# The expert layers' result stores move from SyncE's queue to GpSimd's

## What is computed

```
# layer 0: 8 experts, hidden width 256
u = x @ W1[e];  v = x @ W2[e];  h = u * sigmoid(u) * v;  y = h @ W3[e]
out += y * weights[e]
# layer 1: 16 experts, hidden width 64, and an expert that all tokens share
hidden = silu(x @ gate[e]) * (x @ up[e]);  down = hidden @ down_proj[e]
out += combine[e] * down;   out += silu(x @ sh_gate.T) * (x @ sh_up.T) @ sh_down.T
```

## Time and profile before

| | |
|---|---|
| Time, median of 3 runs | 1060.67 us (1058.96 to 1060.71) |
| Time of the profiled execution | 1064.14 us |
| Span of the profiled execution, first to last instruction | 1062.3 us |
| Busy share of the span: PE, DVE, ACT, POOL | 78%, 61%, 47%, 41% |
| Expert layer 0 | 181.3 to 258.1 us |
| Expert layer 1 | 546.5 to 618.6 us |
| DMA packets and bytes | 68861, 78.93 MB |

### The profile page before, as it was taken

One profiled execution on the slowest core, in us unless ns is written; L12 is line 12 of the kernel. 1 busy time (PEld: TensorE's weight loads), 2 busy tenths in 40 slices (PEclk: granted clock), 3 DMA queues, 4 the chain that ended last, 5 costly groups with the idle time before them and its releaser, 6 DMA issues. The chain is left out here.

```text
span 1062.3 us, 20849 instructions
## 1 busy us (share of the span) xinstructions
PE 825.1 (78%) x5970; PEld 594.1 (56%) x5984; DVE 645.4 (61%) x1891; ACT 500.5 (47%) x1403; POOL 439.7 (41%) x779
## 2 busy tenths in 40 slices
PE   4999882896679999999738849989688456259991
PEld 1556561564457777777516635666467345237771
DVE  5798983333356777777544449999598334334443
ACT  1565661553146666666514626768534122025552
POOL 3356644001424466553320046654255128804344
PEclk9998996899579999999969967999968665579996
DMA  8999700331000000000013420000001211122214
GB/s 268 369 405 346 243 19 29 82 81 46 11 6 12 12 22 21 21 18 9 16 32 76 117 54 20 19 19 9 1 1 46 75 41 37 46 59 57 56 38 130
DMA packets 68861, 78.93 MB, mean 74 GB/s; under 512 B 12432, under 2 KB 58144, under 8 KB 68496
## 3 DMA queue, kind: packets, MB, share of 16 engines
q1 hardware_dynamic: 59840, 62.74, 18.6%
q0 software_dynamic: 6368, 13.38, 4.4%
q10 hardware_dynamic: 2544, 1.48, 0.6%
HBM read 31.61 MB, written 45.96 MB: 73 GB/s over the span
## 5 line engine op out<-in xcount | busy, mean ns | idle before, releaser
L313 POOL DMA_INDIRECT routed_region<-routed_lines,line_slots x96 | 96.5, 1005 | 23.3 <-issue 22.7
L345 POOL DMA_INDIRECT late_results<-routed_region,line_slots x64 | 63.6, 993 | 96.1 <-DVE work_a L624 79.4
L248 POOL TENSOR_TENSOR small<-small,half_and_eps 128x1 f32<-128x1 f32 x160 | 95.1, 594 | 12.5
L753 ACT ACTIVATE probs_keymajor_a<-banks 128x512 f32<-128x512 f32 x128 | 70.1, 595 | 44.9 <-PE banks L556 44.9
L868 PE MATMUL banks<-work_a,weights_a 128*128 128x128 f32 x512 | 79.0, 301 | 14.0 <-ACT work_a L1084 8.2
L1244 PE MATMUL banks<-weights_f,block_feat_f 128*128 x156 | 83.6, 618 | 1.2 <-ACT block_feat_f L1296 0.9
L629 DVE TENSOR_REDUCE small<-banks 128x8 f32<-128x1024 f32 x64 | 77.6, 1212 | 6.4 <-PE banks L530 6.3
L530 PE MATMUL banks<-work_a 32*128 32x512 f32 x256 | 81.0, 712 | 0.0
L868 PEld LDWEIGHTS banks<-work_a,weights_a 128*128 128x128 f32 x512 | 66.6, 203 | 23.2 <-ACT work_a L1084 10.3
L638 DVE TENSOR_TENSOR exps_a<-banks,small 128x1024 f32<-128x1024 f32 x64 | 77.7, 1214 | 2.7 <-PE banks L556 2.4
L556 PE MATMUL banks<-consts,exps_a 128*128 128x128 f32 x512 | 73.5, 290 | 1.3 <-ACT work_a L787 1.3
(11 more groups left out here) (277 smaller groups left out, 2026.6 us busy)
## 6 DMA issues: line engine op xcount, KB each, us to landing
routed_region<-mid_a SPq DMA_DIRECT2D x52, 528.0 KB, 13.4
block_lines_f<-routed_region SPq DMA_DIRECT2D x125, 66.0 KB, 1.9
routed_region<-block_out_f SPq DMA_DIRECT2D x86, 64.0 KB, 1.7
weights_f<-in_weights_f SPq DMA_DIRECT2D x1, 4096.0 KB, 16.9
weights_f<-in_weights_f SPq DMA_DIRECT2D x3, 1024.0 KB, 12.6
shifted_rows<-work_a SPq DMA_DIRECT2D x16, 128.0 KB, 1.7
both_outs_f<-expert_results SPq DMA_DIRECT2D x4, 512.0 KB, 5.7
routed_region<-routed_lines,line_slots POOLq DMA_INDIRECT x96, 2.3
```

The source lines that it names most:

```text
L248: nc.gpsimd.tensor_tensor(rstd[:, s, 1:2], rstd[:, s, 0:1], k.half[:, 0:1], ALU.pow).then_inc(sem.rstd, 1)
L313: nc.gpsimd.indirect_dma_start(k.regions[layer % 2], bass.IndirectOffsetOnAxis(k.slots[:, b, j:j + 1], 0), k.line[:, b % LINES, j, :], Non ...
L345: nc.gpsimd.indirect_dma_start(k.late[:, b % 2, j, :], None, k.regions[layer], bass.IndirectOffsetOnAxis(k.slots[:, b, j:j + 1], 0)).then_ ...
L753: nc.scalar.activation(k.pT[:, g * 512:(g + 1) * 512], bank[:, PT + g % 2, :], ACT.Copy).then_inc(s.pT, 1)
```

## The change

The `store` of SyncE's program goes away, and GpSimd gets a loop that, block by block, waits for the result and stores it by an ordinary (direct) DMA to the same rows, with the same semaphore. GpSimd reads the row numbers into its own registers, eight at a time. SyncE's program is then the loads alone. The last expert layer is as before.

```
-            def store(m):
-                sp.wait_ge(s.y_out, m + 1)
-                sp.dma_start(region[bass.ds(rows_[m], T), 0:D], k.y[:, m % RING, :]).then_inc(ld.stored[m % RING], 16)
-
-            for m in range(nb + RING + 3):
-                if m < nb:
-                    load(m)
-                if linear and m >= RING + 3:
-                    store(m - RING - 3)
+            for m in range(nb):
+                load(m)
...
         @block.gpsimd
         def _(pool):
+            if linear:
+                pool.wait_ge(s.tab, TAB_ROWS)
+                rows_ = []
+                for m in range(nb):
+                    if m % 8 == 0:
+                        c8 = min(8, nb - m)
+                        rows_.extend(registers(mybir.EngineType.Pool, row_i[:, m:m + c8], REGIONS[layer % 2] * SHARE - T))
+                    pool.wait_ge(s.y_out, m + 1)
+                    pool.dma_start(region[bass.ds(rows_[m], T), 0:D], k.y[:, m % RING, :]).then_inc(ld.stored[m % RING], 16)
```

## The result

| | before | after |
|---|---|---|
| Time, median of 20 runs each | 1061.78 us | 1065.89 us |
| Ratio after/before, 95% interval | | 1.0036 (1.0022 to 1.0051) |
| Time of the profiled execution | 1064.14 us | 1061.67 us |
| Expert layer 0: first transpose to last result | 188.3 to 257.41 us | 188.4 to 258.89 us |
| Last result of layer 0 to first gather of attention 1 | 2.55 us | 5.94 us |

The change costs 3.8 us (0.36% of 1061.8, between 2.3 and 5.4). I had forecast 22. One of the changed kernel's 20 runs, a slow one of 1609.3 us, is in its median but not in the ratio; the other 19 lie between 1061.6 and 1069.3 us. The profiled execution is one of the fastest of them, so a comparison stage by stage says more here than the two spans.

A forecast was written before the change was run, and what follows sets the result against it. PE was taken to bound expert layer 0 and SP's queue, by a little, layer 1, where GpSimd would become the bound; 1.9 + 20.2 = +22.1 us on the median 1060.67 gave 1082.8 us, range 1067 to 1096 us.

The forecast's parts named there:

- What a store costs on GpSimd: Both expert layers: a direct store priced like the last layer's scatters, 0.97 us plus a 0.30 us gap, 1.27 us.
- my low bound of 0.66 us: Store on GpSimd: least cost, SP's 0.36 us plus the 0.30 us between two GpSimd DMAs.
- my own sign of being wrong: Profile afterwards: direct DMAs of GpSimd well below 0.9 us, or a drain not holding the barrier, would refute the forecast.
- And becomes the bound: Expert layer 1's loop: GpSimd, slower than PE and SP, sets the pace and the layer ends 20.2 us later.
- the first rival: Both layers: GpSimd's direct store is cheap, no loss; -1.9 us at the low bound, 1058.8 us; chance 0.08.
- What SP gives back: Expert layer 1's loop: SP alone holds back 5.8 us at most; in layer 0 nothing.
- GpSimd is the bound: Expert layer 1's loop: at 1.27 us a store GpSimd is slower than PE's 0.84 and SP's 0.99 us.
- Layer 0's end: From layer 0's last result to attention 1's first gather: gather starts 1.9 us later, bounds +0.6 and +4.5.
- The drain's size: Expert layers' ends: GpSimd's drain adds 2.7 us, as behind attention 0; bounds 0.04 and 5.3 us.
- a drain holds the barrier: Expert layers' ends: GpSimd must drain before signalling; behind layer 0 the barrier opens 3.2 us later for all.
- the stores land under it: Expert layers' ends: the new stores land during GpSimd's 2.7 us drain, so the first gather needn't wait for them.
- the loop of layer 0 stays with PE: Expert layer 0's loop: a 1.27 us store is under PE's 1.64 us turn, so PE still bounds it.

The follow-up runs named there:

- e8: Against the kernel before: expert layer 1's stores all on GpSimd, each cut into two DMAs of 64 rows; layer 0 unchanged; ratio 1.0211 (1.0172 to 1.0251).
- e4: Against the kernel before: only expert layer 0's last store on GpSimd, its other 38 on SP; ratio 1.0030 (1.0009 to 1.0050).
- e9: The changed kernel without GpSimd's drain in the barriers behind the two expert layers; ratio against the kernel before 1.0009 (0.9980 to 1.0037).
- e11: The kernel before, all stores on SP, without GpSimd's drain in the barriers behind attention stages 0, 1 and 2; ratio 0.9927 (0.9900 to 0.9953).

## Why the prediction was wrong

The range was 1067 to 1096 us, the measured time 1065.9; the sign was right and the size wrong by a factor of almost six. That the sign came out right is luck: the predicted loss was to come from layer 1's loop, which got faster, and the measured one stands at the two ends.

- **"What a store costs on GpSimd", the step that failed.** I took the scatters' 0.97 us plus a gap of 0.30, 1.27 us a store. A direct DMA takes 0.54 us, and the gap is 0.06 us where GpSimd is behind (five in 2.92 us); the 0.28 us between rows is waiting for results that come at PE's pace. The step is 0.60 us. That is even below my low bound of 0.66 us, which had kept the scatters' gap. I had argued that the list of rows speaks for somewhat less and the register for somewhat more, and took them to cancel. Together a direct DMA costs 0.43 us less than a scatter; how much of that is the list no run separates. The profile shows my own sign of being wrong, direct DMAs well below 0.9 us.
- **"And becomes the bound", layer 1 at +20.2 us, falls with it.** At a step of 0.60 us GpSimd is faster than PE's 0.84, keeps up and bounds nothing; the five register loads took 0.63 us each and not 1.2. Measured are -4.8 us in the loop and +4.4 at its end, -0.4 in all.
- **The condition stood in the first rival.** It put break-even at a step of 0.80 us, and the measured one is under it, so GpSimd doesn't bind and SP's relief shows. I gave that 0.08. Its price, -1.9 us, was wrong too, because of the ends: -0.4 in layer 1 where it had -3.2, and +3.4 in layer 0 where it had +1.3.
- **"What SP gives back", up to 5.8 us:** measured 4.8 (51.0 against 46.2), of which some 3.0 are waits and 1.8 the clock, which my bound did not name; I had feared a lower clock from a PE that idles more, and it idled less.
- **"GpSimd is the bound" at 1.27 us:** the mechanism is right. e8 had a step of 1.19 us by another road and lost 22.4 us. The nearness to my 22.1 is chance: its drain had 94 DMAs behind it, 7.7 us and not 2.7.
- **Layer 0's end, +1.9 us:** measured +3.4. Of the terms, the store starts 0.64 us behind the result and not 0.1; descriptors take 0.54 and not 0.97; the drain 3.3 and not 2.7; and from the signal to the gather 1.4 us pass instead of 0.7, with 1.02 us of them behind the memset (1.03 in e4). The trace has the reason for a part: GpSimd's queue ends its last semaphore wait of `fetch` at 263.99 us and the gather starts at 264.83, 0.84 us later. In the kernel before it is the same, 0.79 us (259.17 to 259.96); there the waits themselves ended late, with the stores' landing, so that my 0.7 left this step out. What GpSimd does in it is not shown.
- **The drain's size, 2.7 us with 5.3 as a bound:** both rows were at hand, and the scatters of either stage could be counted. 32 and 64 DMAs give the law, and with it 3.2 and 3.9 us for the two layers. I took the second row for a high bound where it was the second point of a line. The third drain of the earlier trace rows, L1159's 4.02 us, would have been its third point, 3.3 us behind the arithmetic for 39 scatters. In the sum this was 0.6 and 1.2 us.
- **That a drain holds the barrier, that the stores land under it, and that the loop of layer 0 stays with PE:** right. From issue to landing a store takes 2.1 us on GpSimd and took 1.7 on SP.
- The Trainium skill's page "DMA: Bandwidth & Descriptors", section "Issuing engines are not separate DMA queues", says that issuing from several engines saves only the sequencer's time to initiate a DMA. The trace of the loop agrees: SP's time was the bound there, and the loop got 4.8 us shorter. The section doesn't mention the stages' ends, which got 7.8 us longer, 6.0 of it gone in e9, which has no drain there.

## What to carry to other kernels

Before work is moved to an idle engine, read what that engine does at the stage's barrier: on GpSimd each DMA (from 32 on) left 0.083 us to be paid at its next drain, however long ago it was issued, and a single late one held the drain for 1.4 us. So give GpSimd the early ones, let another queue take the last few, and put drains (or barriers that include one) where GpSimd waits anyway. A barrier without the drain opened before GpSimd's last DMAs were made, so semaphores have to order those. A price taken from the nearest instruction needs its own range: here scatter and direct copy of the same rows differ by 0.43 us, and the answer turned between them.

## What the runs showed of the hardware

- A direct DMA of GpSimd costs 0.54 us of its time with 128 rows of 512 bytes and 0.53 us with 64; a scatter or gather of 128 rows costs 0.97.
- GpSimd's drain ended 1.4, 1.7, 2.7, 3.3, 3.9, 5.3, 6.5, 7.7 and 8.5 us behind its last work, for 1, 8, 32, 39, 47, 64, 79, 94 and 103 DMAs since its previous drain. From 32 on that is 0.083 us a DMA, for direct ones, scatters and gathers alike, across barriers without a drain (e9, e11), and with 75 us between the DMAs and the drain (attention 2's 32 in e11). Behind a memset alone the drain took 0.19 us.
- The first gather of attention 1 starts 0.8 us behind GpSimd's last semaphore wait in both kernels.
- A register load of eight numbers takes 0.63 us on GpSimd; it took 0.53 on SP, 0.61 on PE and 1.8 on ACT.
